# Unit 13 finished by one scaling in PSUM, and all four engines' calls in a new order

## The reference

```
x = x + layernorm( A( layernorm(x) ) )
x = x + layernorm( F( layernorm(x) ) )
A(h): y = causal depthwise convolution of h along the 256 tokens with
          K[c, t] = C[c] * sigmoid(A_param[c])**t * B[c],  plus D[c] * h
      return layernorm(h + gelu(y) @ W_proj.T + b_proj) * gamma + beta
F(h): hr, hk = mixes of each token with the one before it (mu_r, mu_k)
      return sigmoid(hr @ W_r.T) * (relu(hk @ W_k.T)**2 @ W_v.T)
```

## Time and profile before

| | |
|---|---|
| three runs | 150.49 us median, 150.21 to 150.92 |
| profiled execution | 150.25 us, its span 148.5 us |
| granted TensorE clock, mean | 0.988 |
| busy: PE, DVE, ACT, POOL | 135.5, 130.8, 129.6, 127.5 us |
| moved by DMA | 4.59 MB read, 4.19 MB written |

### The profile page before, as it was taken

The page is one execution under the profiler, slowest core; times in us unless marked ns, Lnnn a source line. Parts: engine busy times, 40 slices in busy tenths (PEclk is TensorE's granted clock), DMA queues, the critical chain, the costliest instruction groups (busy, mean ns, idle before and its releaser), DMA issues.

```text
span 148.5 us, 3239 instructions
## 1 busy us (share of the span) xinstructions
PE 135.5 (91%) x950; PEld 116.0 (78%) x950; DVE 130.8 (88%) x372; ACT 129.6 (87%) x388; POOL 127.5 (86%) x176
## 2 busy tenths in 40 slices
PE   6778888989999999999999999999999999999910
PEld 6667787876988799797979797988887887777900
DVE  0989999999999988999997999998999899339981
ACT  4878999799699999979779999959998988999940
POOL 4599999998989988989896998978999899978282
PEclk9999999999999999999999999999999999999995
DMA  3999900000000002000200002200200200424524
GB/s 89 235 328 272 299 22 0 0 2 0 0 4 0 0 0 77 0 2 0 75 0 0 0 4 71 73 0 7 71 2 0 71 4 0 141 68 138 152 72 141
DMA packets 18705, 8.99 MB, mean 61 GB/s; under 512 B 1536, under 2 KB 18688, under 8 KB 18688
## 3 DMA queue, kind: packets, MB, share of 16 engines
q1 hardware_dynamic: 17840, 8.52, 19.7%
q10 hardware_dynamic: 848, 0.26, 0.7%
HBM read 4.59 MB, written 4.19 MB: 59 GB/s over the span
## 4 chain that ended last, share of the span: by engine, by line
PE 73%; POOL 17%; DVE 4%; DMA 2%; issue 1%; POOLq 1%; ACT 0%
PE ps_k L855 9%; PE ps_k L856 9%; PE ps_r L867 9%; PE ps_r L866 9%; PE ps_tv L876 9%; PE ps_z L833 7%; POOL x_r L227 5%; POOL xn_pow L236 5%; PE ps_tv L846 5%; PE ps_prefix L813 4%; PE ps_z L834 4%; PE ps_xT L805 3%; PE ps_prefix L819 2%; PE ps_prefix L815 2%; DMA a_col<-in_A_param 2%
## 5 line engine op out<-in xcount | busy, mean ns | idle before, releaser
L370 ACT ACTIVATE xn<-x_all,x_bias,x_r 128x128 f32<-128x128 f32 x64 | 26.4, 499 | 1.1 <-POOL x_bias L218 0.6
L867 PE MATMUL ps_r<-mixed_T,tsT 128*128 128x128 f32 x128 | 24.7, 275 | 0.0
L866 PE MATMUL ps_r<-mixed_T,tsT 128*128 128x128 f32 x128 | 24.7, 275 | 0.0
L833 PE MATMUL ps_z<-pv_T,gelu 128*128 128x128 f32 x128 | 22.1, 275 | 0.0
L426 ACT ACTIVATE f_normal<-f,out_bias,yf_r 128x128 f32<-128x128 f32 x48 | 19.8, 493 | 1.5 <-POOL out_bias L285 1.5
L236 POOL TENSOR_TENSOR xn_pow<-xn,pow_token 128x512 f32<-128x512 f32 x16 | 20.3, 1273 | 0.0
L866 PEld LDWEIGHTS ps_r<-mixed_T,tsT 128*128 128x128 f32 x128 | 19.5, 192 | 0.5 <-issue 0.5
L833 PEld LDWEIGHTS ps_z<-pv_T,gelu 128*128 128x128 f32 x128 | 19.4, 191 | 0.5 <-issue 0.5
L389 ACT ACTIVATE junk<-ps_z 128x128 f32<-128x128 f32 x64 | 16.7, 280 | 3.2 <-PE ps_z L834 3.2
L867 PEld LDWEIGHTS ps_r<-mixed_T,tsT 128*128 128x128 f32 x128 | 19.4, 192 | 0.0
L834 PE MATMUL ps_z<-ident,xnT 128*128 128x128 f32 x64 | 17.4, 273 | 0.0
(11 more groups left out here) (112 smaller groups left out, 360.1 us busy)
## 6 DMA issues: line engine op xcount, KB each, us to landing
out_x<-x_all SPq DMA_DIRECT2D x15, 256.0 KB, 2.2
x_all<-in_x SPq DMA_DIRECT2D x7, 512.0 KB, 6.0
x_all<-in_x SPq DMA_DIRECT2D x2, 128.0 KB, 2.8
x_all<-in_x SPq DMA_DIRECT2D x1, 256.0 KB, 3.2
out_x<-x_all SPq DMA_DIRECT2D x1, 128.0 KB, 1.8
out_x<-x_all ACTq DMA_DIRECT2D x1, 128.0 KB, 1.9
w_pv<-in_W_proj ACTq DMA_DIRECT2D x1, 64.0 KB, 2.6
w_pv<-in_W_v ACTq DMA_DIRECT2D x1, 64.0 KB, 4.5
```

The costliest lines, as they stand in the source:

```text
L370: last = a_.activation(tile(xn[u % D], j), xa(u, j), ACT.Identity, bias=col(x_bias, u, j), scale=col(x_r, u, j))
L833: t_.matmul(tile(ps_z[u % 3], j), tile(gelu[u % D], j), pv_T[:, 0, :], start=True, stop=False)
L866: t_.matmul(tile(ps_r, j), tsT[u % D][:, q, l + 1:l + 1 + P], mixed_T[:, 0, :], start=True, stop=False)
L867: last = t_.matmul(tile(ps_r, j), tsT[u % D][:, q, l:l + P], mixed_T[:, 1, :], start=False, stop=True)
```

## The change

It does two things. In unit 13, shift_fused and the single instruction of centre_fused go. A new scale_fused waits for the root of f and then does, per tile and in place in the PSUM bank, (f - mean) * root; add_fused then does (x - scaled mean of y) + that, in one instruction per tile. The semaphore fused_shifted goes with shift_fused.

And the four lists of calls are in a new order. Every call stands once in both, but for shift_fused, centre_fused and scale_fused. The SP queue is as before.

```diff
@@ vector functions
-            def centre_fused():
+            def scale_fused():
 
                 u = FUSED[0]
                 dve.wait_ge(f_stats, u + 1)
-                whole = fused_f[:].rearrange("p (j c) -> p j c", c=P)
-                v_.tensor_tensor(whole, whole, yf_raw[:, u, 1, :, 1:2].to_broadcast([P, TILES, P]),
-                                 ALU.subtract).then_inc(fused_centred, 1)
-
-            def shift_fused():
+                dve.wait_ge(f_r_done, u + 1)
+                for j in range(TILES):
+                    last = v_.tensor_scalar(tile(fused_f, j), tile(fused_f, j), yf_raw[:, u, 1, j, 1:2],
+                                            yf_r[:, u, 1, j:j + 1], ALU.subtract, ALU.mult)
+                last.then_inc(fused_centred, 1)
+
+            def add_fused():
 
                 u = FUSED[0]
+                dve.wait_ge(fused_centred, 1)
                 dve.wait_ge(fused_y_mean, 1)
                 dve.wait_ge(ts_pool_ready, T_ON_POOL.index(u) + 1)
-                dve.wait_ge(t_stats, u + 1)
-                for j in range(TILES):
-                    last = v_.tensor_scalar(xa(u, j), xa(u, j), fused_y[:, j:j + 1], None, ALU.subtract)
-                last.then_inc(fused_shifted, 1)
-
-            def add_fused():
-
-                u = FUSED[0]
-                dve.wait_ge(fused_centred, 1)
-                dve.wait_ge(fused_shifted, 1)
-                dve.wait_ge(f_r_done, u + 1)
-                for j in range(TILES):
-                    last = v_.scalar_tensor_tensor(xa(u, j), tile(fused_f, j), yf_r[:, u, 1, j:j + 1], xa(u, j),
-                                                   ALU.mult, ALU.add)
+                for j in range(TILES):
+                    last = v_.scalar_tensor_tensor(xa(u, j), xa(u, j), fused_y[:, j:j + 1], tile(fused_f, j),
+                                                   ALU.subtract, ALU.add)
                 last.then_inc(out_fused, 1)
```

Parts of the four lists, with the heads and the ends ("..." where calls are left out):

```diff
@@ POOL
-            x_scale_tiles(0, 0, 2)
-            x_scale_tiles(1, 2, 4)
-            x_scale_of(1, 1, 1); xn_times_pow(0); x_scale_of(2, 2, 2); xn_times_pow(1); x_scale_of(3, 4, 2)
-            xn_times_pow(2); xn_times_pow(3); z_root(0, 1); x_scale_of(4, 6, 2)
-            z_root(1, 1); y_variance(0, 1); y_root(0, 1); xn_times_pow(4); x_scale_of(5, 8, 2); y_variance(1, 1)
-            t_variance(0, 1); y_root(1, 1); xn_times_pow(5); t_root(0, 1); z_root(2, 2)
-            xn_times_pow(6); t_variance(1, 1); t_root(1, 1); xn_times_pow(7); y_variance(2, 2); y_root(2, 2)
...
-            add_f(6); add_f(7); f_variance(10, 2); t_variance(15, 1); t_root(15, 1); f_root(10, 2); yf_means(10, 2)
-            out_biases(10, 2); add_f(8); add_f(9); f_variance(12, 2); add_f(10); f_root(12, 2); yf_means(12, 2)
-            out_biases(12, 2); scale_last_y_mean(); f_variance(14, 1); f_root(14, 1); yf_means(14, 1); out_biases(14, 1)
+            x_scale_tiles(0, 0, 2); x_scale_tiles(1, 2, 4); x_scale_of(1, 1, 1); xn_times_pow(0); x_scale_of(2, 2, 2)
+            xn_times_pow(1); xn_times_pow(2); x_scale_of(3, 4, 2); xn_times_pow(3); z_root(0, 1); x_scale_of(4, 6, 2)
+            z_root(1, 1); y_variance(0, 1); xn_times_pow(4); y_root(0, 1); xn_times_pow(5); y_variance(1, 1)
+            y_root(1, 1); t_variance(0, 1); t_root(0, 1); xn_times_pow(6); z_root(2, 2); t_variance(1, 1)
+            t_root(1, 1); scale_t_pool(1); x_scale_of(5, 8, 2); y_variance(2, 2); y_root(2, 2); xn_times_pow(7)
...
+            yf_means(10, 2); t_variance(15, 1); out_biases(10, 2); t_root(15, 1); scale_last_y_mean(); add_f(7)
+            add_f(8); scale_fused_y_mean(); f_variance(12, 2); f_root(12, 2); yf_means(12, 2); out_biases(12, 2)
+            add_f(9); add_f(10); f_variance(14, 1); f_root(14, 1); yf_means(14, 1); out_biases(14, 1)
@@ ACT
-            normalise(0); load_w_v(); copy_xT(0); normalise(1); make_mixers(); normalise(2); gelu_of(0); copy_xT(1)
...
-            relu_k(14); copy_tT(15); scale_f_late(11); square_k(14); tanh_r(14); relu_k(15); square_k(15)
-            scale_f_late(12); tanh_r(15); scale_f(14); store_last_half()
+            normalise(0); normalise(1); load_w_v(); copy_xT(0); make_mixers(); normalise(2); gelu_of(0); copy_xT(1)
+            normalise(3); copy_w_rk(); square_z(0); gelu_of(1); copy_xT(2); normalise(4); square_z(1); gelu_of(2)
...
+            square_z(9); normalise(14); copy_tT(5); square_k(4); tanh_r(4); normalise(15); copy_xT(12); scale_t(6)
...
+            relu_k(14); copy_tT(15); square_k(14); scale_f_late(11); tanh_r(14); scale_f_late(12); relu_k(15)
+            square_k(15); tanh_r(15); scale_f(14); store_last_half()
@@ DVE
-            x_stats(2); x_pooled(2, 2); x_stats(4); x_pooled(4, 2); convolve(0); x_stats(6); keep_pv()
...
-            t_stats_of(15); gate(12); f_stats_of(12); gate_fused(); stats_fused(); shift_fused(); centre_fused()
-            add_f_late(11); add_fused(); subtract_y_mean(); gate(14)
-            f_stats_of(14); add_f_late(12); gate_half(0); f_stats_half(0); gate_half(1); f_stats_half(1)
-            centre_half(0); add_f_half(0); centre_half(1); add_f_half(1)
+            x_stats(2); x_pooled(2, 2); x_stats(4); x_pooled(4, 2); convolve(0); keep_pv(); x_stats(6); x_pooled(6, 2)
...
+            t_stats_of(14); f_stats_of(10); f_stats_of(11); residual(15); gate(12); t_stats_of(15); gate_fused()
+            f_stats_of(12); stats_fused(); subtract_y_mean(); scale_fused(); add_f_late(11); gate(14); f_stats_of(14)
+            add_fused(); gate_half(0); f_stats_half(0); gate_half(1); f_stats_half(1); add_f_late(12); centre_half(0)
+            centre_half(1); add_f_half(0); add_f_half(1)
@@ PE
-            keep_busy(3); transpose_xn(0); keep_busy(6); prefix_sum(0); keep_busy(6); transpose_pv(); transpose_xn(1); prefix_sum(1)
-            project(0); transpose_xn(2); prefix_sum(2); project(1); transpose_xn(3); transpose_rk(); prefix_sum(3)
-            mix_weights(); transpose_xn(4); project(2); prefix_sum(4); project(3); transpose_xn(5); prefix_sum(5)
-            project(4); transpose_t(0); transpose_xn(6); prefix_sum(6); keys(0); gates(0); prefix_sum(7)
...
-            gates(14); keys(15); values(14); gates(15); values(15)
+            centre_bias(); keep_busy(3); transpose_xn(0); keep_busy(6); prefix_sum(0); keep_busy(6); transpose_pv()
+            transpose_xn(1); prefix_sum(1); transpose_rk(); project(0); prefix_sum(2); transpose_xn(2); project(1)
+            transpose_xn(3); prefix_sum(3); project(2); mix_weights(); transpose_xn(4); prefix_sum(4); project(3)
+            prefix_sum(5); transpose_xn(5); project(4); transpose_t(0); prefix_sum(6); keys(0); transpose_xn(6)
+            transpose_t(1); gates(0); keys(1); transpose_xn(7); values(0); prefix_sum(7); project(5); gates(1)
...
+            gates(14); values(14); keys(15); gates(15); values(15)
```

More of the change, by code:

```diff
@@ L334, in _ @@
[L334 to L338, removed]
@@ L339, in _ @@
-            z_root(10, 2); add_f(2); t_root(8, 2); add_f(3); y_variance(10, 2); f_variance(4, 2)
-            y_root(10, 2); scale_t_pool(9); f_root(4, 2); yf_means(4, 2); out_biases(4, 2); t_variance(10, 2)
-            z_root(12, 2); add_f(4); t_root(10, 2); scale_t_pool(10); y_variance(12, 2)
-            f_variance(6, 2); y_root(12, 2); f_root(6, 2); yf_means(6, 2); z_root(14, 1)
-            out_biases(6, 2); scale_t_pool(11); t_variance(12, 2); t_root(12, 2); add_f(5)
-            z_root(15, 1); y_variance(14, 1); f_variance(8, 2); y_root(14, 1); f_root(8, 2); yf_means(8, 2)
@@ new lines, in _ @@
+            f_variance(0, 1); scale_t_pool(3); y_variance(4, 2); y_root(4, 2); f_root(0, 1); xn_times_pow(10)
+            x_scale_of(7, 12, 2); z_root(6, 2); t_variance(4, 2); t_root(4, 2); f_variance(1, 1); xn_times_pow(11)
+            yf_means(0, 1); scale_t_pool(5); y_variance(6, 2); y_root(6, 2); xn_times_pow(12); out_biases(0, 1)
+            x_scale_of(8, 14, 2); f_root(1, 1); xn_times_pow(13); t_variance(6, 2); z_root(8, 2); t_root(6, 2)
+            f_variance(2, 2); yf_means(1, 1); f_root(2, 2); y_variance(8, 2); out_biases(1, 1); y_root(8, 2)
@@ new lines, in _ @@
+            scale_t_pool(7); yf_means(2, 2); out_biases(2, 2); add_f(0); t_variance(8, 2); xn_times_pow(14)
+            xn_times_pow(15); z_root(10, 2); add_f(1); t_root(8, 2); f_variance(4, 2); add_f(2); y_variance(10, 2)
+            y_root(10, 2); scale_t_pool(9); f_root(4, 2); yf_means(4, 2); out_biases(4, 2); add_f(3); z_root(12, 2)
+            f_variance(6, 2); t_variance(10, 2); t_root(10, 2); f_root(6, 2); yf_means(6, 2); y_variance(12, 2)
+            y_root(12, 2); scale_t_pool(10); out_biases(6, 2); scale_t_pool(11); add_f(4); z_root(14, 1)
@@ new lines, in _ @@
+            t_variance(12, 2); t_root(12, 2); add_f(5); y_variance(14, 1); z_root(15, 1); y_root(14, 1)
+            f_variance(8, 2); f_root(8, 2); y_variance(15, 1); yf_means(8, 2); out_biases(8, 2); scale_t_pool(13)
```

(12 more changed lines are left out.)

85 lines of the change are left out of this document (35 added, 50 removed).

## The result

The changed kernel takes 149.38 us (median of six runs, 149.28 to 149.78), the kernel before beside it 150.45 us (six runs). The ratio is 0.9929, with a 95% interval of 0.9912 to 0.9947: 1.1 us faster. In a later session the same kernel gave 149.35 against 150.49 us, ratio 0.9919 [0.9904, 0.9935]. I had forecast 148.4 us: faster, as it came, but with a gain of 2.1 us where 1.1 us is there. The profiled execution took 149.28 us, with a span of 147.2 us, 1.3 us less than before.

A forecast was written before the change was run, and what follows sets the result against it. PE, closed from 30.39 to 138.79 us, was taken as the bound. Span 148.5 - (145.90 - 144.05) + 0.1 = 146.75 us, plus 1.75 around it: 148.5; 0.24 and 0.25 cancel, forecast 148.4 us, range 147.4 to 150.0.

The forecast's parts named there:

- the case that I held likeliest: The whole kernel takes 147.5 to 148.9 us, crowded last stores included; chance 0.62.
- (a): At the start W_v lands at 14.2 and convolve(1) starts 1.2 us late: 149.1 us, chance 0.17.
- (b): A thin margin fails in the middle, the lead is lost, 0.5 of the tail remains: 149.75 us, chance 0.14.
- The size of the lead: At the start on PE, project(4) begins at 30.2 instead of 31.81: 1.6 us; t_root(0) on POOL ends at 29.4.
- The step on W_v: Load issue moves behind normalise(1) on ACT; weights land between 13.0 and 14.2; low end taken, 0.1 us lost on PE.
- The finish at nothing: Unit 13's new finish saves DVE 1.5 us, costed at nothing because its operations move behind a wait for f_root(12).
- the walk: Call-by-call estimate of the new lists through four engines; it had the last store at 143.8, 0.25 ahead of the sums.
- The cover: POOL's add_f(9) and add_f(10), until 137.9, hide the later gate(14); without them 1.1 us would stand ahead of it.
- The port pair: DVE's subtract_y_mean meets f_variance(12) and f_root(12) on POOL; if POOL loses, f_root(12) starts up to 0.9 us late.
- rival (c): On ACT, relu_k(15) queues behind a late scale_f_late(12), with the root held 1.3 us: 151.45 us, chance 0.07.
- The tail: At the end, the last store is issued near 144.05, before at 145.90; its landing stretches by 0.1 us.
- Rival (d): At the end, crowded last stores end last: up to 0.5 us more; no separate chance, counted within the 0.62.
- The middle: PE never waits in the closed stretch and its lead stands between 1.5 and 1.8 us; thinnest margin 0.2 us.

The follow-up runs named there:

- e4_order: The changed kernel's new lists with the old finish of unit 13 (shift_fused and centre_fused in place of scale_fused): 149.17 us, ratio 0.9918 to the kernel before.
- e10_cover: The kernel before with the new finish of unit 13 and POOL's add_f(10) moved behind out_biases(12): 151.04 us, ratio 1.0041 to the kernel before.
- e8_early12: The new order with the old finish of unit 13, and add_f_late(12) on DVE moved ahead of unit 15's halves: 149.04 us, ratio 0.9901 to the kernel before.
- e1_head: The kernel before with only the heads of the four lists new, up to scale_t_pool(1), scale_t(0), y_stats_of(3) and transpose_t(0): 153.81 us, ratio 1.0209.
- e5_start: The kernel before with the new start, cut where all four engines have issued the same calls in both orders: 149.92 us, ratio 0.9958.
- e9_one_call: The kernel before with one POOL call, x_scale_of(5), moved behind t_root(1): 151.39 us, ratio 1.0067.
- e11_no_tail: The changed kernel with the old order of the tail and the old finish: 149.44 us, ratio 0.9942 to the kernel before.

## Why the prediction was right or wrong

**The place of the gain: right.** I said that PE's closed stretch begins sooner, keeps its lead, and that the tail adds a little. The lead at the last row is 1.14 of the 1.3 us that the span lost, and one call put back takes all of the gain away.

**The range: hit, but not by the case that I held likeliest.** 149.38 us lies inside 147.4 to 150.0, but outside 147.5 to 148.9, the case to which I gave 0.62. It lies between the times of rivals (a) and (b), and neither of them happened in the profiled execution. That the range reached up to (b) is what made it hold.

**The size of the lead: too large by 0.46 us, and this is the error in the span** (147.2 measured, 146.75 forecast). t_root(0) ends at 29.88, not 29.4, project(4) begins at 30.74, not 30.2. The step on W_v was misread. I took the low end of its landing and 0.1 us for PE, because the call behind the transpose had begun at 13.11. But that was the start of another call; PE is at the transpose itself at 11.9, as every profile with the old place shows. The weights came at 12.0 to 12.9, earlier than my low end of 13.0, and PE waited for them in five of the eight profiles with the new place. In the profile of the result it did not: there x(2) came late, and POOL stood idle for 0.47 us ahead of x_scale_of(2), which began at 10.18 instead of 9.84. The sum has no term for that. With the load put back and x(2) in time, t_root(0) ends at 29.59 and project(4) begins at 30.45; of the 0.54 us that were missing there, 0.29 are gone. In what is left, 0.25, project(3) begins at 27.14, 0.09 later than the sum has it, and takes until project(4) 3.31 us, where the three terms of the sum (1.33, 1.4 and 0.45) give 3.18. So rival (a), late weights, is real in other executions, at 0.15 to 0.50 us of project(4) where I gave it 0.7, but it is not what took the lead in this one.

**The finish at nothing: right, with little to spare, and the condition was priced wrong.** DVE waits 1.60 us for f_root(12), which ended at 135.62, 0.8 us later than in the walk, and scale_fused took 1.38 us, the high end of 1.1 to 1.4. Together they put gate(14) 0.87 us behind where the old finish lets it begin (e4_order). The cover that I named was add_f(9) and add_f(10). They ended at 138.81, not 137.9, and POOL still waited 0.36 us for unit 14's statistics behind them. In e4_order it waits for nothing there, but then 0.42 us for the statistics of the first half. From PE's last row to the last store it is 4.49 and 4.50 us: the two covers together hide the delay. I wrote that without the cover 1.1 us would stand ahead of gate(14). Without it, in the old order, it was 1.66: not the instructions of scale_fused but the wait that they bring, with everything queued behind it on DVE.

**The port pair: it falls on POOL, and it is small.** subtract_y_mean kept its 0.86 us for four while f_variance(12) and then f_root(12) began beside it. f_ve took 0.28 us and the root began 0.43 us after it; in e10_cover, where DVE stood idle beside the same two calls, it was 0.20 and 0.35. So POOL lost 0.1 us. The Trainium skill, "SBUF — State Buffer", "Who interferes with whom", has the one that issues second wait for the whole of the other's instruction; DVE's instructions here are four of 0.28 us, and by that POOL can lose at most one of them each time, not the 0.9 us that I allowed. With that bound the trace agrees. With the other half of the rule it does not. In e4_order the root runs from 134.04 to 135.72 us, and four instructions of the form that once took 1303 ns start inside it, at 134.14 to 134.73, and take 0.28 us each; e8_early12 shows the same. In e1_head, e5_start, e9_one_call and e11_no_tail, where POOL's 512-element add runs beside them, one of the four takes 1297 to 1304 ns. So, with the kernel before, the long hold came with the add in five traces and with the root in none, and that a root is held for 1.3 us, as rival (c) had it, no run shows.

**The tail: the sum right by two errors.** From PE's last row to the last store I had 4.71 us (140.94 less 1.6 to 144.05) and 2.70 of landing, together 7.41; measured are 4.49 and 2.91, together 7.40. f_variance(14), which I had at 138.1, began at 139.17, still 1.7 us earlier than before and ahead of the halves. Rival (d), the crowded last stores, came true with 0.3 of its up to 0.5 us. out_biases(12) ended at 136.35, 0.95 later than the walk had it but ahead of the 137.8 from which rival (c) decides; relu_k(15) began at 137.94, ahead of 138.5.

**The middle: right for this order.** No wait of PE is listed from 30.39 to 138.79, and the lead grows from 1.07 to 1.14 us, so rival (b) did not come. How near it was, e5_start shows: with the old middle most of the lead in its trace is lost, in waits that the timeline does not bracket.

**Around the span** the profiled execution had 2.08 us where I took 1.75. The medians are 2.02 over the first six runs of the changed kernel, 1.81 over the next six and 1.77 over 17 runs of the kernel before. About 0.1 of this may be real, the rest is spread. And the walk's 0.25 us, which I subtracted, was not there: the sums from rows were nearer than the call-by-call walk. Of the 0.98 us between 148.4 and 149.38, 0.46 is lead, 0.25 the walk, 0.09 that 148.49 was rounded down to 148.4, and the other 0.2 lies in the time around the span and in the spread of the executions.

**A version that may beat both kernels** is the new order with the old finish and add_f_late(12) ahead of the halves (149.04 us beside 149.35 for the changed kernel in the same session); another is the changed kernel with W_v's load back (148.92, in another session). In both cases the interval overlaps that of the changed kernel, so neither is shown to be faster than it. The two edits touch different ends of the kernel. The two together were not run.

## What to carry to other kernels

When one engine is closed for most of the span, look for what lets its closed stretch begin sooner, and then test whether the order behind it can keep the lead; a call moved alone, without the calls on other engines that feed and use it, can turn the gain into a loss. A call that waits late in an in-order list costs its wait and all that is queued behind it, so price the wait and not only the instructions. In the tail, count from the last row of the bounding engine to the last store and from there to the end separately: a store that is issued earlier beside three others lands less early than it was issued: 1.61 us became 1.3 here.

## What the runs showed of the hardware

- Waits of up to 0.2 us of PE stood in no bracket and in no list of waits, as a matmul's modelled end covers them. They show as a longer first row (1.13 instead of 1.02 us, 0.46 instead of 0.39) and in the distance of starts.
- In e1_head, PE was idle for 2.6 of the 29.6 us from 30.39 to 60, with 1.94 us in one wait that ended at 41.17. The mean granted clock was 1.00 from 30.39 to 40 us, 0.83 from 40 to 50 and 1.00 again behind it, so a part of the middle window ran at the 1.2 GHz level; the changed kernel and the one before show 1.00 throughout. That the 3.4 us lost are more than PE's idle time fits this; it was not tried apart.
- A DMA on ACT's queue was issued with the first activation of the call ahead of it, not behind its last: 8.54 us, beside the activation at 8.53, in the trace of after.
- Four two-step DVE operations with a per-partition mean and root, 128x128 in PSUM, took 1.38 us from first start to last end, 0.41 for each by itself, against 0.86 and 0.28 for four with one step in SBUF (scale_fused and subtract_y_mean in the trace of after).
- A one-step DVE operation of 128x128 in SBUF took about 1300 ns in five traces where POOL's add of 128x512 began just before it, and 278 to 284 ns in two traces where POOL's root of 128x8 ran beside it from start to end (e4_order, e8_early12).
